# First layer norm in halves, with the loads reordered and the first weight splits moved between engines

## The reference

```python
x = x + L0_attn(_layernorm(x), up_w, gate_w, local_point, local_approx_output, fuse_weight, discount, ffn_*)
# L0_attn(h), S = 128 columns:
approx_up = h @ up_w.T                      # (.., 128)
delta = h @ gate_w.T - local_point          # (.., 128)
out = approx_up @ local_approx_output.T     # Taylor term 0
for m in 1..6:                              # Taylor terms 1 to 6
    dterm = |delta|**m * exp(-discount[m-1]) (signed for odd m; for m > 4 kept only where |delta| <= 2.5)
    out += (dterm * approx_up) @ fuse_weight[:, :, m-1].T
out += (silu(h @ ffn_gate_w.T) * (h @ ffn_up_w.T)) @ ffn_down_w.T
```

## Time and profile before

| | us |
|---|---|
| median of three runs (lowest, highest) | 2455.73 (2455.06, 2457.9) |
| the profiled execution, its own time | 2459.67 |
| its span, from first to last instruction | 2457.8 |
| mean granted TensorE clock, as a share of full | 0.987 |
| TensorE busy / VectorE / ScalarE / GpSimd | 2358.6 / 1255.9 / 902.7 / 668.3 |
| first instruction of VectorE that is not a semaphore | 12.27 |
| first product of TensorE with a weight | 39.15 |

### The profile page before, as it was taken

One profiled execution on the slowest core, in us unless ns is written; L12 is line 12 of the kernel. 1 busy time (PEld: TensorE's weight loads), 2 busy tenths in 40 slices (PEclk: granted clock), 3 DMA queues, 4 the chain that ended last, 5 costly groups with the idle time before them and its releaser, 6 DMA issues.

```text
span 2457.8 us, 38454 instructions
## 1 busy us (share of the span) xinstructions
PE 2358.6 (96%) x13227; PEld 2012.9 (82%) x13227; DVE 1255.9 (51%) x2921; ACT 902.7 (37%) x2232; POOL 668.3 (27%) x383
## 2 busy tenths in 40 slices
PE   4999899999999999998999999999999999998788
PEld 3788688888888888987888888888888888887455
DVE  6444644444444444446554444444444444457766
ACT  2111344444444444443233333333333333334764
POOL 4334522322222232221231111111111111112542
PEclk9999999999999999999999999999999999999889
DMA  3110211211111111110111111111111111110000
GB/s 117 63 48 26 103 52 51 78 58 51 68 51 51 65 71 51 51 68 27 45 54 45 45 45 44 38 40 37 37 38 43 45 45 45 45 54 1 1 1 35
DMA packets 36832, 118.97 MB, mean 48 GB/s; under 512 B 4905, under 2 KB 7337, under 8 KB 36785
## 3 DMA queue, kind: packets, MB, share of 16 engines
q1 hardware_dynamic: 36784, 118.35, 14.1%
HBM read 116.24 MB, written 2.10 MB: 48 GB/s over the span
## 4 chain that ended last, share of the span: by engine, by line
PE 88%; DVE 5%; issue 3%; POOL 2%; ACT 1%; SPq 0%; DMA 0%; POOLq 0%; ACTq 0%; DVEq 0%
PE pj L542 19%; PE pj L543 19%; PE pj L544 19%; PE ou L542 6%; PE ou L544 6%; PE ou L543 6%; PE pv L720 2%; PE sc L857 2%; PE pv L866 2%; PE sc L704 2%; PE tp L711 1%; POOL w_lo L410 1%; POOL w_hi L408 1%; PE sc L969 1%; DVE neg_max L1938 1%
## 5 line engine op out<-in xcount | busy, mean ns | idle before, releaser
L402 POOL TENSOR_TENSOR w_lo<-raw,w_hi 128x1024 fp32r<-128x1024 f32 x145 | 346.7, 2391 | 1441.2 <-ACT w_hi L1104 1401.8
L542 PE MATMUL pj<-xt_hi,w_hi 128*128 128x512 f32 x1232 | 499.8, 406 | 6.6 <-DVE xt_lo L1473 2.4
L543 PE MATMUL pj<-xt_lo,w_hi 128*128 128x512 f32 x1232 | 483.1, 392 | 0.0
L544 PE MATMUL pj<-xt_hi,w_lo 128*128 128x512 f32 x1232 | 482.3, 392 | 0.0
L542 PEld LDWEIGHTS pj<-xt_hi,w_hi 128*128 128x128 f32 x1232 | 233.5, 190 | 51.1 <-issue 3.1
L542 PE MATMUL ou<-w_hi,act_hi 128*128 128x512 f32 x684 | 274.5, 401 | 0.8 <-DVE x L1397 0.6
L544 PEld LDWEIGHTS pj<-xt_hi,w_lo 128*128 128x128 f32 x1232 | 232.6, 189 | 49.7
L544 PE MATMUL ou<-w_hi,act_lo 128*128 128x512 f32 x684 | 267.6, 391 | 0.0
L543 PEld LDWEIGHTS pj<-xt_lo,w_hi 128*128 128x128 f32 x1232 | 233.6, 190 | 40.9
L543 PE MATMUL ou<-w_lo,act_hi 128*128 128x512 f32 x684 | 266.9, 390 | 0.0
L1397 DVE TENSOR_TENSOR x<-x,ou 128x512 f32<-128x512 f32 x192 | 130.8, 684 | 247.1 <-PE ou L544 246.8
(11 more groups left out here) (242 smaller groups left out, 4538.9 us busy)
## 6 DMA issues: line engine op xcount, KB each, us to landing
raw<-in_l1a_w SPq DMA_DIRECT2D x80, 512.0 KB, 4.1
raw<-in_l0x_w SPq DMA_DIRECT2D x64, 512.0 KB, 4.3
side<-in_side SPq DMA_DIRECT2D x32, 512.0 KB, 4.0
raw<-in_ffn_w SPq DMA_DIRECT2D x15, 512.0 KB, 3.3
raw<-in_l0f_w SPq DMA_DIRECT2D x6, 512.0 KB, 3.7
raw<-in_l1x_w SPq DMA_DIRECT2D x6, 512.0 KB, 3.8
raw<-in_taylor_w SPq DMA_DIRECT2D x5, 512.0 KB, 6.9
x<-in_x SPq DMA_DIRECT2D x2, 1024.0 KB, 6.4
```

The source lines that it names most:

```text
L402: pool.tensor_tensor(WL[:, s, :], RAW[:, s, :], f32(WH[:, s, :]), ALU.subtract).then_inc(w_ready[s], 1)
L542: pe.matmul(out, wh, xh, start=first, stop=False)
L543: pe.matmul(out, wh, xl, start=False, stop=False)
L544: return pe.matmul(out, wl, xh, start=False, stop=last)
```

## The change

Nothing is computed differently; order and engines change.

- SyncE: the identity has its own semaphore and goes first; then the first half of x, weight piece 0, the second half of x, the eleven other constants, pieces 1 to 4. `x_in` becomes one semaphore for each half.
- VectorE and ScalarE do the layer norm in halves. Rows use four `PR` buffers. ScalarE writes `WH` of piece 0 and VectorE its `WL`, after the first four rows. VectorE does statistics and rows 4 to 7 after that, waits for `consts_in` only before the Taylor terms, and for `ce_ready` later still.
- The `pj` fills are renumbered: rows 0 to 3 are fills 0 to 3, the first half's projections fills 4 and 5, rows 4 to 7 fills 6 to 9, the second half's projections fills 10 and 11. So TensorE projects the first half before it turns rows 4 to 7, and row 4's transposes need the bank that the first `keep` gives back. VectorE's `XTL` of rows 4 to 7 comes after the first half's `keep`.
- GpSimd waits for all eight rows (`ln_x`), then splits pieces 1 to 4. Ffn pieces 1 and 2 are split during the second half of the Taylor products (`ta_used` 8 and 10), the cross attention's first piece after `ta_used` 12, its second after the last Taylor product.

```diff
--- before.py
+++ after.py
@@ -46,7 +46,7 @@
 OU_ORDER = ["taylor", "ffn", "l0x", "l0f", "l1a", "l1x", "l1f"]
 
 
-CONSTS_IN = ["identity", "local_point", "discount", "bias", "lora_keys", "lora_wq", "expert_rows", "norm_w",
+CONSTS_IN = ["local_point", "discount", "bias", "lora_keys", "lora_wq", "expert_rows", "norm_w",
              "one", "block_mask", "q3", "q3_norm"]
 
 
@@ -90,7 +90,10 @@
 NG = B * KVH // KG
 
 
-LNV = [0, 1, 3, 5, 7, 9]
+LNV = [0, 2, 4, 6, 8, 10]
+
+
+LN0_FILL, TAYLOR_FILL = [0, 1, 2, 3, 6, 7, 8, 9], [4, 5, 10, 11]
 LT = [None, 0, B, 2 * B]
 
 SLOT = dict(
@@ -209,8 +212,8 @@
         ou = [psum("ou0"), psum("ou1")]
 
 
-        consts_in, x_in, fs_in, mask_in = sem("consts_in"), sem("x_in"), [sem("fs_in0"), sem("fs_in1")], sem("mask_in")
-        dt_in, out_done = sem("dt_in"), sem("out_done")
+        consts_in, x_in, fs_in, mask_in = sem("consts_in"), [sem("x_in0"), sem("x_in1")], [sem("fs_in0"), sem("fs_in1")], sem("mask_in")
+        dt_in, out_done, identity_in = sem("dt_in"), sem("out_done"), sem("identity_in")
         w_in = [sem(f"w_in{s}") for s in range(NSLOT)]
         ta_used = sem("ta_used")
         w_hi = [sem(f"w_hi{s}") for s in range(NSLOT)]
@@ -312,7 +315,7 @@
         query_banks = [ou[0], ou[1], pv, ou[0]]
 
         block = ctx.enter_context(nc.Block())
-        CONSTS = [IDN[:], LP[:], DC[:], BIAS[:], KEYS[:], LQ[:], SEL[:], NW[:], ONE[:], BM[:], Q3[:], QN[:]]
+        CONSTS = [LP[:], DC[:], BIAS[:], KEYS[:], LQ[:], SEL[:], NW[:], ONE[:], BM[:], Q3[:], QN[:]]
 
 
         @block.sync
@@ -329,12 +332,17 @@
                     sp.wait_ge(c_ready, c - 1)
                 sp.dma_start(FSF[:, (c % 2) * T:(c % 2 + 1) * T], a["ctx_t"][c]).then_inc(c_in[c % 2], 16)
 
-            for n in range(2):
+            def load_x(n):
                 sp.dma_start(X[:, n * HB:(n + 1) * HB, :],
-                             a["x"][n * HB:(n + 1) * HB].rearrange("b p d -> p b d")).then_inc(x_in, 16)
+                             a["x"][n * HB:(n + 1) * HB].rearrange("b p d -> p b d")).then_inc(x_in[n], 16)
+
+            sp.dma_start(IDN[:], a["identity"]).then_inc(identity_in, 16)
+            load_x(0)
+            load(0, 0, a["taylor_w"][0])
+            load_x(1)
             for dst, name in zip(CONSTS, CONSTS_IN):
                 sp.dma_start(dst, a[name]).then_inc(consts_in, 16)
-            for s in range(NSLOT):
+            for s in range(1, NSLOT):
                 load(s, 0, a["taylor_w"][s])
             sp.dma_start(MI[:], a["mask"]).then_inc(mask_in, 16)
             for s in range(3):
@@ -419,13 +427,15 @@
 
 
             pool.wait_ge(consts_in, 16 * len(CONSTS))
-            for s in range(NSLOT):
+            pool.wait_ge(ln_x, B)
+            for s in range(1, NSLOT):
                 split(s, 0)
 
-            for s in range(3):
-                split(s, SLOT["ffn"][s], (ou_full, OU["taylor"] + B) if s else (pj_full, PJ["taylor"] + 4))
-            for s in L0X_SLOTS[:2]:
-                split(s, SLOT["l0x"][s])
+            split(0, SLOT["ffn"][0], (pj_full, PJ["taylor"] + 4))
+            for s in range(1, 3):
+                split(s, SLOT["ffn"][s], (ta_used, TAYLOR - 1 + 2 * s))
+            split(3, SLOT["l0x"][3], (ta_used, 2 * (TAYLOR - 1)))
+            split(4, SLOT["l0x"][4], (ou_full, OU["taylor"] + B))
             with pool.Fori(1, FG) as i:
                 split(0, i + SLOT["ffn"][0], (pj_full, i * 8 + (PJ["ffn"] - 1)))
                 split(1, i + SLOT["ffn"][1], (pj_full, i * 8 + PJ["ffn"]))
@@ -610,12 +620,24 @@
                 pe.wait_ge(w_ready[s], k + 1)
 
 
+            def fill0(k):
+                return PJ["ln0"] + k, k % 2
+
+            pe.wait_ge(identity_in, 16)
+            for hf in range(2):
+                for b in range(hf * HB, (hf + 1) * HB):
+                    n, bank = fill0(LN0_FILL[b])
+                    pe.wait_ge(ln_x, b + 1)
+                    pj_free(n)
+                    for c in range(KC):
+                        last = pe.transpose(pj[bank][:, c * P:(c + 1) * P], PR[:, b % 4, c * P:(c + 1) * P], IDN[:])
+                    last.then_inc(pj_full, 1)
+                if hf == 0:
+                    ready(0, 0)
+                pe.wait_ge(pj_done, PJ["ln0"] + LN0_FILL[hf * HB + HB - 1] + 1)
+                for j in range(2):
+                    project(fill0(TAYLOR_FILL[2 * hf + j]), wcols(0, j), wide(XT, hf))
             pe.wait_ge(consts_in, 16 * len(CONSTS))
-            layer_norm(0)
-            ready(0, 0)
-            for hf in range(2):
-                for j in range(2):
-                    project(nth(PJ["taylor"], 0, 0, 2 * hf + j), wcols(0, j), wide(XT, hf))
 
             for hf in range(2):
                 for m in range(TAYLOR):
@@ -1103,9 +1125,19 @@
                 act.wait_ge(w_hi[s], k)
                 act.activation(WH[:, s, :], RAW[:, s, :], ACT.Copy).then_inc(w_hi[s], 1)
 
+            def rows0_hi(hf):
+                for b in range(hf * HB, (hf + 1) * HB):
+                    n = PJ["ln0"] + LN0_FILL[b]
+                    hi((n, n % 2), XTH[:, :, b * S:(b + 1) * S], pj[n % 2][:].rearrange("p (c s) -> p c s", c=KC))
+
+            half_deviation(0, 0)
+            act.wait_ge(w_in[0], 16)
+            act.activation(WH[:, 0, :], RAW[:, 0, :], ACT.Copy).then_inc(w_hi[0], 1)
+            rows0_hi(0)
+            half_deviation(0, 1)
             act.wait_ge(consts_in, 16 * len(CONSTS))
             act.activation(CE[:], DC[:], ACT.Exp, scale=-1.0).then_inc(ce_ready, 1)
-            layer_norm(0)
+            rows0_hi(1)
             for hf in range(2):
                 for m in range(TAYLOR):
                     if hf:
@@ -1523,11 +1555,35 @@
             dve.sem_inc(pv_done, 1)
             dve.sem_inc(sx_nm, B)
             dve.sem_inc(la_sqa, 2)
-            dve.wait_ge(x_in, 32)
-
-
-            dve.wait_ge(ce_ready, 1)
-            layer_norm(0)
+            def rows0_stats(hf):
+                dve.wait_ge(x_in[hf], 16)
+                for b in range(hf * HB, (hf + 1) * HB):
+                    dve.bn_stats(ST[:, b, :], X[:, b, :]).then_inc(ln_stat, 1)
+                half_deviation(0, hf)
+
+            def row0(b):
+                dve.tensor_scalar(PR[:, b % 4, :], X[:, b, :], MV[:, b, 0:1], RS[:, b:b + 1],
+                                  ALU.subtract, ALU.mult).then_inc(ln_x, 1)
+
+            def row0_lo(b):
+                n = PJ["ln0"] + LN0_FILL[b]
+                at = (slice(None), slice(None), slice(b * S, (b + 1) * S))
+                lo((n, n % 2), HI["ln0"] + b, XTL[at], pj[n % 2][:].rearrange("p (c s) -> p c s", c=KC), XTH[at])
+
+            rows0_stats(0)
+            half_rstd(0, 0)
+            for b in range(HB):
+                row0(b)
+                if b:
+                    row0_lo(b - 1)
+            row0_lo(HB - 1)
+            dve.wait_ge(w_hi[0], 1)
+            dve.tensor_tensor(WL[:, 0, :], RAW[:, 0, :], f32(WH[:, 0, :]), ALU.subtract).then_inc(w_ready[0], 1)
+            rows0_stats(1)
+            half_rstd(0, 1)
+            for b in range(HB, B):
+                dve.wait_ge(pj_full, PJ["ln0"] + LN0_FILL[b - HB] + 1)
+                row0(b)
 
             def taylor_outputs(hf):
                 for b in range(HB):
@@ -1537,10 +1593,13 @@
 
             for hf in range(2):
                 up, delta, keep = TY[0], TY[1], TY[2]
-                n0, bank0 = nth(PJ["taylor"], 0, 0, 2 * hf)
+                n0 = PJ["ln0"] + TAYLOR_FILL[2 * hf]
+                bank0 = n0 % 2
                 dve.wait_ge(pj_full, n0 + 1)
                 if hf:
                     dve.wait_ge(ta_lo, TAYLOR)
+                else:
+                    dve.wait_ge(consts_in, 16 * len(CONSTS))
                 dve.tensor_copy(up, pj[bank0][:]).then_inc(ta_t, 1)
                 dve.wait_ge(pj_full, n0 + 2)
                 dve.wait_ge(ta_t, hf * TAYLOR + 1)
@@ -1550,6 +1609,10 @@
                 dve.wait_ge(pj_done, n0 + 1)
 
                 dve.scalar_tensor_tensor(keep, delta, 2.5, keep, ALU.is_le, ALU.mult).then_inc(pj_done, 1)
+                if hf == 0:
+                    for b in range(HB, B):
+                        row0_lo(b)
+                    dve.wait_ge(ce_ready, 1)
                 if hf:
                     taylor_outputs(0)
                 for m in range(TAYLOR):
```

## The result

Six runs of the changed kernel have a median of 2446.23 us (2444.58 to 2449.64), six of the kernel before 2457.13 (2455.06 to 2457.9): a ratio of 0.9956, 95% interval 0.9945 to 0.9967. The profiled execution took 2446.34 us with a span of 2444.4, at a mean granted clock of 0.985.

A forecast was written before the change was run, and what follows sets the result against it. TensorE, busy for 96% of the span, bounds the kernel, so only its idle time can be won: 8.0 (head) - 1.0 (held lows) + 1.8 (ffn wait) = 8.8 us, from 2455.73 to 2446.9 us, range 2440.5 to 2452.5.

The forecast's parts named there:

- rival A: Whole change as summed, VectorE held once per GpSimd instruction: 2446.9 us, 2443.5 to 2450.5; chance 0.65.
- signs: In the new profile: first `keep` over 1 us, second over 2, two short `act_lo` waits in the first Taylor half.
- The start: Kernel head: x's first half lands at 6.55, rows from 10.1, first product at 18.6 instead of 39.15.
- C: Loads at the start: transfers share the engines, x's first half lands 4 us later; 2450.9 us; chance 0.06.
- The first two products: First half's projections: 6.9 us for the pair, second product ending at 25.5; 6.9 also for third and fourth.
- The `keep` and the transposes: Between second and third product: GpSimd holds both `keep`, which end at 28.4 and 31.0; third product at 36.4.
- The Taylor chain: First Taylor half: VectorE held, TensorE waits for lo 1 and lo 2; half ends at 64.0, 8.0 us won.
- The second half: Taylor's second half: ffn splits inside it hold VectorE's lows, 1.0 us lost, bounds 0 and 1.5.
- The ffn wait: Before the second ffn product: the 1.83 us wait for GpSimd's `w_lo` goes, 1.8 us won.
- Sum: Whole kernel: 8.0 - 1.0 + 1.8 = 8.8 us won, from a median of 2455.73 to 2446.9 us.
- Rival B: Head: the locking does not reach the path, first Taylor half ends at 57.6 to 59.0; 2439.5 to 2441 us; chance 0.12.
- D: Head: VectorE held through GpSimd's whole run, third product at 47.7; 2.2 us slower, 2457.9 us; chance 0.07.

The follow-up runs named there:

- e12: The changed kernel once more, with no edit; 2448.68 us, ratio 0.9965 to the kernel before.
- e9: e8 plus ScalarE's high parts of pieces 1 to 4, GpSimd's low parts of 2 to 4 behind the second `keep`, spare transposes; 2448.50 us, ratio 0.9968.
- e10: The changed kernel with loads in the old order: x, identity, other constants, then weight pieces; 2446.53 us, ratio 0.9952.
- e6: The changed kernel with spare transposes of the identity put where TensorE waits; 2445.63 us, ratio 0.9958.
- e7: The changed kernel with the edits of e5 and e6 together; 2438.15 us, ratio 0.9931.
- e11: The same kernel as e7, run again in more rounds; 2437.91 us, ratio 0.9919.
- e5: e4 with GpSimd's low part of piece 1 at once and those of pieces 2 to 4 behind the second `keep`; 2440.20 us, ratio 0.9931.
- e3: The changed kernel with the ffn and cross attention splits behind the last Taylor product, as before; 2449.53 us, ratio 0.9967.
- e1: The kernel before, with its first layer norm started without waiting for the constants; 2454.29 us, ratio 0.9986.
- e8: The changed kernel without its halves: all eight rows ahead of all four projections; 2448.20 us, ratio 0.9970.
- e2: The changed kernel with GpSimd splitting pieces 1 to 4 as soon as they land, not behind the eighth row; 2451.67 us, ratio 0.9979.
- e4: The changed kernel with ScalarE writing the high parts of pieces 1 to 4 and GpSimd only the low parts; 2444.16 us, ratio 0.9944.

## Why the prediction was right, point by point

The forecast was 2446.9 us, the median 2446.23; in the second series, e12, it was 2448.68 beside a kernel before of 2456.63. The mechanism was rival A's, but the agreement to a microsecond is luck. The forecast stood on a median of 2455.73 us from three runs, which six runs put at 2457.13, so the gain by medians is 10.9 us, and 8.0 in the second series, where 8.8 was forecast. And the 8.8 is itself the sum of errors with opposite signs. Two of the signs that I had named did not appear: the first `keep` took 0.80 us, not over 1 (1.15 in e12), and no wait for `act_lo` came in the first Taylor half.

- **The start.** x's first half was there at 7.1, not 6.55, and the transfers did finish one after the other, so C is out: the landings of the two halves release `bn_stats` at 7.13 and, in e9, at 11.10. Rows from 10.71 (predicted 10.1), `w_lo` done at 19.0 (18.5), first product 19.07 (18.6). e10 shows the order of loads worth 1.4 to 1.6 us.
- **The first two products.** Sized at 6.9 us, they took 8.59, and the third and fourth 8.18. This term was too small by 3.0 us in all. I had taken the old first pair's figure; e6, e7 and e11 show that for the first pair idle time ahead of it is the cause. The old pair followed transposes that were spread over 16 us and a wait of 0.45 us, the new one transposes over 5 us and a wait of 2.54.
- **The `keep` and the transposes.** Held as said, 0.80 and 2.26 us, and the third product at 36.60 (36.4), though the second product ended 2.2 later than predicted: the first `keep` met GpSimd's instruction nearer its end (GpSimd had started at 24.67, predicted 23.7) and waited 0.4 us instead of 1.7. e5, in which neither is held, has it at 33.81.
- **The Taylor chain.** I predicted two waits for `act_lo` of 0.6 and 1.1 us; there were none. GpSimd's ffn piece 0 waits for the fourth product, which the slow matmuls made late (44.78), so GpSimd paused from 43.2 to 45.1 and VectorE got three instructions in. In e6, where the products start earlier and are faster, GpSimd has no pause and the wait is there at 2.14 us. The first half ended at 63.98, predicted 64.0: the start was 0.5 late and the matmuls slow by 3.0, against some 2.0 of the phase at `keep` and 1.5 of waits that did not come. That these cancel is chance.
- **The second half.** The 1.0 us for held lows was wrong: in e12 VectorE was held (2.20, then the last two lows in 5.18 us), and the half still took 17.34 us, as it does before the change. VectorE was further ahead than I had counted: the low before the held ones was out 6.5 us after the start of the half, not 8.5, and the last one 13.9 after it, not 17.2. The changed kernel's first trace lost 1.6 us there, but to the clock, at 0.91 and with no wait.
- **The ffn wait.** 1.83 us, gone, and back in e3.
- **Sum.** GpSimd's first split behind the stage, before, after, and in e12:

```profile
116.16 1.89 POOL L408 TENSOR_TENSOR w_hi<-raw,one 128x1024 fp32r<-128x1024 f32 x1 [4.43 <-PE pj L544]
```

```profile
107.51 1.89 POOL L416 TENSOR_TENSOR w_hi<-raw,one 128x1024 fp32r<-128x1024 f32 x1 [14.43 <-PE pj L554]
```

```profile
105.77 1.89 POOL L416 TENSOR_TENSOR w_hi<-raw,one 128x1024 fp32r<-128x1024 f32 x1 [10.75 <-PE pj L554]
```

  The first trace is 8.65 us ahead, against the 8.8 of the sum, but only because its clock cost 1.6 us where 1.0 for held lows stood. Term by term, e12 has 8.3 (predicted 8.0), 0 (minus 1.0) and 2.1 (1.8), together 10.4. The first trace's lead then grows to 11.6 at L720's group (1103.32 and 1091.72) and 13.4 by spans, in stretches where its clock is 0.98 against 0.95 and 0.96. In e12 the lead is 10.4 at that group and 10.9 by spans (2457.8 and 2446.9): only 0.5 comes to it in the rest of the kernel. So the program's own gain is 8.7 to 10.4 us, by what the clock does in the head, and what the first trace has beyond that did not come again with the same code. The medians, 10.9 and 8.0 us apart in the two series, lie around it.
- **What earns it.** The sum did not ask which part of the change earns the 8.0. At the second Taylor half (74.12 before, 65.97 and 65.85 after) the early start alone has 4.0 us (e1), and all parts but the halves have 8.5 (e8). The halves, which give the change its name, add next to nothing on their own: 0.6 and 0.3 us at the third product (36.60 and 36.90 against 37.23), and that is gone at the second Taylor half, as e8's third and fourth product took 7.20 us and not 8.18 and 7.77.

Rival B falls with e5 (whose `keep` are 0.43 and 0.69) and the rows at 28.48 and 29.32; D too, since no instruction lost more than one turn on the path. The range held less of B than I had said: it begins at 2440.5 us, and B was 2439.5 to 2441. By the Trainium skill (TensorE: Matmul & The Clock Gate, Part 1) the same kernel can show a different number of slow matmuls from run to run, as the chip's watch over TensorE's activity doesn't start with the kernel. The traces agree: in two traces of the changed kernel the first 24 matmuls took 8.59 and 8.23 us, and one and the same group 0.68 and 1.19.

## What to carry to other kernels

Time a helper engine's work not by when it is needed but by what runs beside it: against e5, the third product came 8.1 us later when GpSimd's instructions met VectorE's rows (e2) and 2.8 to 3.1 later when they met the two `keep` (the changed kernel's two traces); beside instructions that read PSUM they cost nothing. e5 also gives GpSimd half the work, but that alone gained nothing at this place (e4). A reordering that shortens the way to the first matmul (here by 7 us, e8) is worth only what is left when the next wait is counted, and a change of several parts is to be taken apart before one part gets the credit. And gains of 1 to 3 us in a kernel of this length are to be read from marks in the trace and from more than one trace, as the head moved by 2.8 us between two traces of one kernel (e7 and e11), 1.8 of it the clock in two products.

## What was not expected of the hardware

- Slow matmuls at the start are not in the granted clock's column: 1.00 over 19.07 to 27.66, with starts 0.43 us apart for over half of it.
- Where the clock falls is not fixed by the program. Two traces of the same code have it from 66.0 us on and not at all, and behind the same idle 2.26 us in one and not in the other.
- Holding does not pin a chain in time, it spaces it out: with the start 3.2 us earlier (9.08 against 12.27), all held rows of e1 came 3.9 us earlier.
- Spare transposes bring back nearly all of the rate at the start, 5.89, 5.89 and 5.79 us for the first 24 matmuls (e6, e7, e11) against 7.5 to 8.6 without (7.2 in e9, where they all lie ahead of a wait of 5.26 us). Later it is not every time: 6.32, 5.57, 7.39 and, in e9, 5.57 for the next 24, against 6.9 to 8.2.
